# Attention scores and values in TensorE tiles of 64 rows by 32 columns, with two value banks and a ring of two score slots

## The reference, cut to what matters

```python
xn = layernorm(x)                                  # x: 4 x 2048 x 256
# two attentions of 8 heads of 16 columns, on two halves: xn itself and xn smoothed over time
scores = einsum('bshd,bthd->bhst', q, k) / sqrt(16)
o = einsum('bhst,bthd->bshd', softmax(scores), v)
x1 = layernorm(xh + o @ wo.T + bo);  x2 = the same on the smoothed half
y = concat([x1, x2])
first = layernorm(y + relu(y @ w_ff1.T + b_ff1) @ w_ff2.T + b_ff2)
second = relu(xn @ W1 + b1) @ W2 + b2
out = x + first + second
```

## Time and profile before

| | |
|---|---|
| time, median of 3 runs | 2540.47 us (2539.70 to 2545.86) |
| time of the profiled execution | 2538.24 us |
| its span in the trace | 2536.7 us |
| granted TensorE clock, mean | 0.991 |
| busy: PE, ACT, DVE, POOL | 2457.0, 2183.5, 1346.2, 327.5 us |
| exp (line 722) | 2048 instructions, 1904.7 us |
| values (line 1463), scores (line 1437), portions (line 1224, f16) | 1068.0, 621.4 and twice 214.7 us of PE |

### The profile page before, as it was taken

One profiled execution on the slowest core, in us unless ns is written; L12 is line 12 of the kernel. 1 busy time (PEld: TensorE's weight loads), 2 busy tenths in 40 slices (PEclk: granted clock), 3 DMA queues, 4 the chain that ended last, 5 costly groups with the idle time before them and its releaser, 6 DMA issues.

```text
span 2536.7 us, 66464 instructions
## 1 busy us (share of the span) xinstructions
PE 2457.0 (97%) x29057; PEld 965.5 (38%) x29057; DVE 1346.2 (53%) x3046; ACT 2183.5 (86%) x2419; POOL 327.5 (13%) x293
## 2 busy tenths in 40 slices
PE   6899999999999999999999999999999999999996
PEld 4233333336633333334653333333564333333354
DVE  5344445556744444555684444444677444445566
ACT  5899999986499999997569999999656999999952
POOL 1100110003400020000340002000053001100042
PEclk9999999999999999999999999999999999999998
DMA  8200220006110030000611004000151001200001
GB/s 221 80 10 10 37 40 12 6 6 128 51 60 10 10 61 10 10 6 12 138 50 44 10 10 61 10 10 6 51 99 51 10 10 27 44 10 10 6 30 43
DMA packets 49255, 95.94 MB, mean 38 GB/s; under 512 B 7468, under 2 KB 32044, under 8 KB 48572
## 3 DMA queue, kind: packets, MB, share of 16 engines
q1 hardware_dynamic: 42940, 77.12, 11.4%
q0 software_dynamic: 6016, 14.49, 4.1%
HBM read 57.45 MB, written 34.08 MB: 36 GB/s over the span
## 4 chain that ended last, share of the span: by engine, by line
PE 85%; DVE 10%; ACT 2%; issue 1%; POOL 1%; DMA 1%; SPq 0%; DVEq 0%; ACTq 0%; POOLq 0%
PE slot L1463 33%; PE slot L1437 19%; PE slot L1224 16%; PE slot L1496 6%; PE slot L1512 5%; DVE rden L857 2%; PE slot L1342 2%; DVE hid_one L889 1%; PE slot L1351 1%; DVE rs L771 1%; DVE rden L850 1%; DVE den L852 1%; POOL p_sb L601 1%; PE slot L1289 1%; ACT p_sb L722 1%
## 5 line engine op out<-in xcount | busy, mean ns | idle before, releaser
L722 ACT ACTIVATE p_sb<-slot 128x1024 f32<-128x1024 f32 x2048 | 1904.7, 1031 | 76.2 <-PE slot L1437 76.2
L1463 PE MATMUL slot<-p_sb,v_sb 128*17 128x512 f32 x8192 | 1068.0, 596 | 8.4 <-ACT p_sb L722 8.1
L1437 PE MATMUL slot<-q_st,k_st 50*128 50x512 f16 x4096 | 621.4, 382 | 5.4 <-ACT p_sb L722 3.2
L1437 PEld LDWEIGHTS slot<-q_st,k_st 50*128 50x128 f16 x4096 | 117.1, 94 | 874.3 <-ACT p_sb L722 870.6
L901 DVE SCALAR_TENSOR_TENSOR second<-slot,second 128x256 f32<-128x256 f32 x64 | 27.2, 425 | 593.0 <-PE slot L1224 593.0
L1463 PEld LDWEIGHTS slot<-p_sb,v_sb 128*17 128x17 f32 x8192 | 181.3, 96 | 226.3 <-ACT p_sb L722 208.2
L889 DVE TENSOR_SCALAR hid_one<-slot,b_grown 128x256 f32<-128x256 f32 x256 | 123.8, 483 | 238.6 <-PE slot L1224 236.5
L1224 PE MATMUL slot<-xt_parts,w_parts 128*32 128x256 f16 x6144 | 214.7, 274 | 13.0 <-DVE hid_one L889 13.0
L1224 PE MATMUL slot<-w_parts,hid_parts 128*32 128x256 f16 x6144 | 214.7, 274 | 0.0
L1224 PEld LDWEIGHTS slot<-xt_parts,w_parts 128*32 128x32 f16 x6144 | 140.7, 96 | 125.7 <-issue 95.4
L601 POOL TENSOR_TENSOR p_sb<-area,p_sb 128x512 f16<-128x512 f32 x128 | 149.1, 1166 | 291.1 <-ACT p_sb L738 284.8
(11 more groups left out here) (119 smaller groups left out, 1692.4 us busy)
## 6 DMA issues: line engine op xcount, KB each, us to landing
part_dram<-p_sb SPq DMA_DIRECT2D x16, 1024.0 KB, 4.2
xn<-x SPq DMA_DIRECT2D x16, 512.0 KB, 6.1
second<-x SPq DMA_DIRECT2D x32, 256.0 KB, 2.9
ffn_dram<-second SPq DMA_DIRECT2D x32, 256.0 KB, 2.0
area<-ffn_dram SPq DMA_DIRECT2D x16, 512.0 KB, 4.9
out<-area SPq DMA_DIRECT2D x15, 512.0 KB, 3.3
k_st<-part_dram SPq DMA_DIRECT2D x24, 256.0 KB, 12.0
k_st<-part_dram POOLq DMA_DIRECT2D x48, 128.0 KB, 5.1
```

Source lines behind the costliest of these rows:

```text
L722: act.activation(p_sb[:, n % 4, :], slot[n % 3][:, :], ACT.Exp, scale=0.25 / GROW ** 2).then_inc(exp_done, 1)
L1437: mm = pe.matmul(slot[at % 3][:, k * CHUNK:(k + 1) * CHUNK], k_st[rows_, pair, kt * P:(kt + 1) * P], q_st[rows_, pair, c_ * CHUNK:(c_ + 1) ...
L1463: mm = pe.matmul(o_bank[ROW * j:ROW * j + DK + 1, :], v_sb[:, a, kt, GH * g + j, :], p_sb[:, n % 4, (j % 2) * CHUNK:(j % 2 + 1) * CHUNK], ...
```

## The change

The scores and the values are cut into tiles of 64 rows by 32 columns. A score tile is made by eight matmuls (two row halves by four column groups of 32 keys) in place of two. The values of a kt are eight matmuls in place of four: for each of four heads one on keys 0 to 63 and one on keys 64 to 127, and the two halves go to two banks, `o_banks`, the two halves of slot 2. So slots 0 and 1 alone are the ring for scores: score tile n waits for exp n-2. PE's order in a kt becomes: first score tile of the next kt, portion, second score tile, values. `evict` must add the two banks: a copy of one to `rden`, an add of the other, which then frees the banks, and the shuffle from SBUF. In the prologue the third smoothing waits for `o_read`, and its order changes; in the last batch the first transpose waits for `o_read`.

The three small changes: the loads of the maxima for the next batch go from SP's queue to POOL's (`next_max`); the bias `b_ff2` is added on POOL ahead of `finish` (`bias_y`) and no longer in it; and the scaling in `finish` (line 949 to 956) is done in eight SCALAR_TENSOR_TENSORs of 256 columns instead of four small and two wide ones.

```diff
-            o_bank, side = slot[3][:, 0:CHUNK], slot[3][:, CHUNK:]
+            o_banks, side = [slot[2][:, r * CHUNK:(r + 1) * CHUNK] for r in range(2)], slot[3][:, CHUNK:]
...
-                        act.activation(p_sb[:, n % 4, :], slot[n % 3][:, :], ACT.Exp, scale=0.25 / GROW ** 2).then_inc(exp_done, 1)
+                        act.activation(p_sb[:, n % 4, :], slot[n % 2][:, :], ACT.Exp, scale=0.25 / GROW ** 2).then_inc(exp_done, 1)
...
-                    dve.stream_shuffle(o_sb[:, n % 2, :], o_bank, O_ROWS[n % 2]).then_inc(o_read, 1)
+                    step(dve.tensor_copy(rden[:, :], o_banks[0]))
+                    step.settle()
+                    dve.tensor_tensor(rden[:, :], o_banks[1], rden[:, :], ALU.add).then_inc(o_read, 1)
                     hold(dve, o_read, u + 2)
+                    step(dve.stream_shuffle(o_sb[:, n % 2, :], rden[:, :], O_ROWS[n % 2]))
+                    step.settle()
...
-                        step(dve.tensor_tensor(o_part, o_part, rows("b_ff2", CT // halves), ALU.add))
+                        rows_ = [o_all[:, t, :] for t in range(tiles.start, tiles.stop)]
+                        statistics(rows_)
+                        rsqrt(len(rows_))
+                        for i, row in enumerate(rows_):
+                            step(dve.scalar_tensor_tensor(row, row, mv[:, i, 0:1], c("gamma_ff"), ALU.subtract, ALU.mult))
...
+                        for i, row in enumerate(rows_):
+                            step(dve.scalar_tensor_tensor(row, row, rs[:, 1, i:i + 1], x4[:, tiles.start + i, :], ALU.mult, ALU.add))
...
+                        pe.wait_ge(exp_done, UNITS2 * STEPS * b + at - 1 + 3)
+                        pair = GH // 2 * g + n
+                        for r in range(P // ROW):
+                            for k in range(2):
+                                rows_ = slice(HALF * k, HALF * k + ROWS)
+                                mm = pe.matmul(slot[n][ROW * r:ROW * (r + 1), k * CHUNK:(k + 1) * CHUNK],
+                                               k_st[rows_, pair, kt * P + ROW * r:kt * P + ROW * (r + 1)],
+                                               q_st[rows_, pair, c_ * CHUNK:(c_ + 1) * CHUNK], start=True, stop=True, skip_group_check=True)
...
+                        for j in range(GH):
+                            n = 2 * kt + j // 2
+                            for r in range(2):
+                                rows_ = slice(HALF * r, HALF * (r + 1))
+                                mm = pe.matmul(o_banks[r][ROW * j:ROW * j + DK + 1, :], v_sb[rows_, a, kt, GH * g + j, :],
+                                               p_sb[rows_, n % 4, (j % 2) * CHUNK:(j % 2 + 1) * CHUNK],
+                                               start=(kt == 0), stop=(kt == TILES - 1), skip_group_check=True)
...
+                            if more:
+                                scores(at)
                             if kt in net_kts:
                                 (second_out_part if unit % 2 else second_hidden)(b, unit // 2, net_kts.index(kt))
                             if kt == PROJECTION_KT and unit > 0 and unit % 2 == 0:
                                 out_projection(b, unit - 1)
...
+                            if more:
+                                scores(at + 1)
+                            values(unit, kt)
```

More of the change, by code:

```diff
@@ L594, in first_y, with next_max, bias_y @@
                     pool.tensor_tensor(y4, y4, rows("beta", CT), ALU.add).then_inc(y_ready, 1)
+                def next_max(b):
+                    hold(pool, m_out, 16 * (2 * b + 1))
+                    fill_max(pool, 0, ALL_PAIRS, m_next_in)
+                def bias_y(b, cc):
+                    y4 = resid[:, CT * cc:CT * (cc + 1), :]
+                    pool.wait_ge(yt_rounded, CHUNKS * b + cc + 1)
+                    pool.tensor_tensor(y4, y4, rows("b_ff2", CT), ALU.add).then_inc(y_biased, 1)
                 def nets(b):
@@ L948, in finish @@
                             dve.wait_ge(ff_half_read, 1)
[L949 to L952 removed]
+                        rows_ = [o_all[:, t, :] for t in range(tiles.start, tiles.stop)]
[3 more added lines that the diff above has]
+                            step(dve.scalar_tensor_tensor(row, row, mv[:, i, 0:1], c("gamma_ff"), ALU.subtract, ALU.mult))
                         step.settle()
                         dve.wait_ge(back_in, 16 * (n + 1))
[L956 removed]
+                        for i, row in enumerate(rows_):
+                            step(dve.scalar_tensor_tensor(row, row, rs[:, 1, i:i + 1], x4[:, tiles.start + i, :], ALU.mult, ALU.add))
+                        step.settle()
+                        dve.sem_inc(o_ready if last_part else o_half_ready, 1)
                         if last_part:
@@ L1242, in second_hidden @@
                     h = HALVES * b + i
+                    if i == 0 and k == 0:
+                        pe.wait_ge(ff_read, CHUNKS * b + 2)
                     if k == 4 and i > 0:
@@ L1323, in smooth @@
                     def smooth(k):
+                        if k == 2 and before is not None:
+                            pe.wait_ge(o_read, UNITS2 * b + 1)
                         if k % 2 == 0:
@@ L1417, in attention, with scores @@
                 def attention(b):
-                    def scores(unit, kt):
+                    def scores(at):
+                        unit, kt, n = at // STEPS, at % STEPS // 2, at % 2
                         a, g, c_ = PAIRED_UNITS[unit]
-                        if kt == 0 and c_ == 0:
+                        if at % STEPS == 0 and c_ == 0:
                             if a == 1:
@@ L1427, in scores @@
                                 else:
-                                    hold(pe, q_next_in, 16 * Q_LOADS * b)
-                        for n in (2 * kt, 2 * kt + 1):
-                            at = STEPS * unit + n
-                            pe.wait_ge(exp_done, UNITS2 * STEPS * b + at - 2 + 3)
-                            if at == 2:
-                                pe.wait_ge(ff_read, CHUNKS * b + 1)
-                            for k in range(2):
-                                pair, rows_ = GH // 2 * g + n % 2, slice(HALF * k, HALF * k + ROWS)
-                                mm = pe.matmul(slot[at % 3][:, k * CHUNK:(k + 1) * CHUNK], k_st[rows_, pair, kt * P:(kt + 1) * P],
-                                               q_st[rows_, pair, c_ * CHUNK:(c_ + 1) * CHUNK], start=True, stop=True)
-                            mm.then_inc(scores_made, 1)
@@ L1441, in attention @@
-                    scores(0, 0)
-                    for unit, (a, g, c_) in enumerate(PAIRED_UNITS):
-                        u = UNITS2 * b + unit
+                                    hold(pe, q_next_in, 16 * 2 * len(Q_PART) * b)
+                                    hold(pe, m_next_in, 16 * 2 * b)
+                        pe.wait_ge(exp_done, UNITS2 * STEPS * b + at - 1 + 3)
[6 more added lines that the diff above has]
+                                               q_st[rows_, pair, c_ * CHUNK:(c_ + 1) * CHUNK], start=True, stop=True, skip_group_check=True)
@@ L1444, in attention @@
+                    scores(0)
+                    scores(1)
+                    for unit in range(UNITS2):
                         net_kts = OUT_KTS if unit % 2 else HIDDEN_KTS if unit else FIRST_HIDDEN_KTS
                         for kt in range(TILES):
-                            if kt + 1 < TILES:
-                                scores(unit, kt + 1)
-                            elif unit + 1 < UNITS2:
-                                scores(unit + 1, 0)
+                            at = STEPS * unit + 2 * kt + 2
+                            more = at < UNITS2 * STEPS
+                            if more:
+                                scores(at)
```

40 lines of the change are left out of this document (20 added, 20 removed).

## The result

The changed kernel takes 2667.49 us (median of four runs, 2663.57 to 2672.11) where the kernel before takes 2540.09 (2538.83 to 2545.86): a ratio of 1.0502, interval 1.0485 to 1.0520, so 127 us more. The profiled execution took 2664.47 us, which is 126.2 above that of before.

The account below looks back on a forecast made before the run. PE and ACT are both full in attention, with ACT stopping briefly for PE's score tiles. Terms 33 + 18 + 32 + 3.3 + 1.7 - 2.6 = +85 us on 2538.24 give 2623.6, median 2626; eight-in-ten range 2550 to 2700.

Parts of the forecast that it names:

- Faster: Attention: fewer layout changes end ACT's stops, new waits don't reach ACT, exps keep 0.917; 2474 us, chance 0.12.
- No change: Attention: free layout change, part of even boundary waits and all odd ones absorbed; 2540 within 8, chance 0.04.
- Tiles in turn: Score tiles: halves or column groups wait for each other's loads, 0.44 a tile; 2873 us, chance 0.08 wholly or in part.
- the forecast's own: Whole kernel: the range of the main forecast alone, 2580 to 2660 us, held with chance 0.76.
- Ring of two and order: Attention kts: the second score tile behind the portion makes ACT starve, 7.53 us per four kts against 7.40; +33 us.
- the walk: Step-by-step timing of PE and ACT through four kts (plain, portion, plain, portion), which gave a cycle of 7.53 us.
- estimate of 0.10: PE: a layout change between 128 by 32 portion and 64 by 32 score tile costs 0.10, nothing as lower bound.
- Wait for the eviction in odd units: Boundary into odd units: PE waits 0.56 for copy and add (1.41) before o_read, 32 times; +18 us.
- DVE's chain in even units: Boundary into even units: DVE's late shuffle moves hidden_half 1 and the third portion by 1.15, 28 times; +32 us.
- Prologue: Three prologues: DVE's state copies end later behind the eviction, PE's step goes 1.1 later each; +3.3 us.
- Last batch and tail: End of kernel: last-batch transposes wait for the eviction, +1.7 us; finish gets shorter by its new scaling, -2.6 us.
- well under 479: Attention stage: sign that the forecast is right, PE's busy time falling well below 479 us.

Follow-up runs that it names:

- e9: The kernel before with only the change's two-slot score ring and PE order, old tiles and old eviction: 2669.65 us, ratio 1.0500.
- e5: The kernel before with only the change's eviction (copy, combine, then shuffle), score tiles, order and ring as they were: 2592.45 us, ratio 1.0198.
- e1: The changed kernel with hidden_half 1 ahead of the first reciprocal and hidden_half 2 ahead of the second on DVE: 2645.7 us, ratio 1.0414.
- e2: The changed kernel with a third value bank, so that PE waits for the eviction's copy alone: 2652.67 us, ratio 1.0455.
- e4: The changed kernel with the stack refill's loads spread over the kts by waits on pv_done, not all at once: 2652.71 us, ratio 1.0441.
- e12: The changed kernel with the third portion of an even unit one kt later: 2658.22 us, ratio 1.0453.
- e3: The changed kernel with all four smoothing steps of the prologue ahead of the wait for the state: 2654.04 us, ratio 1.0439.
- e8: The changed kernel with third value bank, smoothing first, spread refill loads, and hidden_half 1 ahead of both reciprocals: 2604.78 us, ratio 1.0238.
- e11: The kernel before with the third portion of an even unit one kt later and the three small changes: 2526.24 us, ratio 0.9939.
- e7: The kernel before with only the three small changes (maxima loads on POOL, bias on POOL, scaling pairs in finish): 2534.73 us, ratio 0.9977.
- e6: The kernel before with hidden_half 1 ahead of both reciprocals on DVE: 2545.98 us, ratio 1.0017.
- e10: The kernel before with the third portion of an even unit one kt later: 2529.32 us, ratio 0.9944.

## Why the prediction was right, and where its sizes were off

The direction and the mechanism were right: all three rivals fall. *Faster* needed copy and add in under 0.87, and they took 1.41. *No change* needed a free change of layout, and it took 0.10. *Tiles in turn* needed 0.44 per score tile, and it took 0.22. The sum was +85 and the profiled difference is 126: the time lies inside the wide range of 2550 to 2700, and above the forecast's own of 2580 to 2660. By its terms:

- **Ring of two and order**, +33: the cycle is 7.57 and not 7.53. (In the walk the first late exp is late by 0.03 and not 0.05; the end at 5.17, with which it goes on, is right.) Before, an odd unit of four cycles was 29.63, so 7.41 each: 256 x 0.16 = +41. The two parts in it are now apart: order and ring alone make the cycle 7.96 (e9), the equal tiles bring it to 7.57. The estimate of 0.10 for the change between portion and score tile held (0.77 for 0.67). The Trainium skill, "TensorEngine Tiling (Array Packing)", Tiling Modes, says that a change of mode drains the engine whichever the modes; the rows of e9 and of the changed kernel agree, 0.10 to 0.12 for each pair that they show.
- **Wait for the eviction in odd units**, +18: 30.86 - 4 x 7.57 = 0.58 a unit, 32 x 0.58 = +19.
- **DVE's chain in even units**, 1.15 each and +32: an even unit takes 32.96 (median), which is 2.68 above its four cycles of 7.57; before it was 30.88 - 29.63 = 1.25 above them. So 1.43 each, 28 x 1.43 = +40. This step was mis-sized. The same eviction in the old order costs 1.18 (e5), which is the 1.15 of the prediction (757.11 - 756.00 is 1.11; a gap of 0.04 behind the shuffle makes it 1.15). The other 0.25 is there only with the change. DVE's chain from the copy to `hidden_half` 1 is as long there as in e5 (7.64 and 7.65), but PE stops at the third portion for 1.22 and not for 0.96. From the values that the eviction lets go to this portion it is 798.33 - 792.10 = 6.23, less the stop 5.01; in e5 776.87 - 770.63 = 6.24, less the stop 5.28. So PE is there 0.27 sooner: one score tile of 0.22, not two, stands ahead of the portion. The prediction moved the portion and the tile behind it by the 1.15 of DVE, and did not count that PE comes sooner. No run changes the order alone at this place.
- **Prologue**, +3.3: +19. This step failed. The delay of DVE's copies is nearly as forecast (1.33 of stop; 1.4 a prologue in e5), but 1.1 us of lateness was taken as 1.1 us of time. The one prologue without a fall of the clock grew by 2.3; the two with one took 7.6 more each; 3 x 2.3 + 2 x 7.6, less the 3.2 of the fall in the kernel before, are the 19. What makes the falls so long is not settled. With the stop and the new order of the smoothing (the changed kernel, e1, e2, e4, e12) the clock fell in 10 of 15 prologues, for 13.7 or 17.1 us; with the same stop and the old order (e5) in 2 of 3, for 6.8; without the stop (e3, e8) in 3 of 6, for 10.2. So the order, which the prediction counted as nothing, seems to have a part in it.
- **Refill**, not in the sum: +9. The prediction counted what the matmuls take to run and not that 20480 more of them, with their loads, must be fetched (160 more packets of 16 KB). e4 shows the cause by taking away the burst in front of the fetch.
- **Last batch and tail**, +1.7 and -2.6: +1.2. Up to PE's last matmul the tail is 2.9 longer: the clock stays low for 6.8 us at its start where it was 3.4 before, which is about 1.7, and the rest is the eviction's. Behind that matmul it is 1.7 shorter, and 1.2 and 1.4 in the kernels with the small changes alone (e11, e7): the 2.6 was too much, since a pair of SCALAR_TENSOR_TENSORs takes 0.88 and pairs have gaps of up to 0.29 ahead of them.

These are 41 + 19 + 40 + 19 + 9 + 1 = 129, 3 above the measured 126. The 41 counts the 16 cycles of the batches' first units with +2.6, but those units became 0.8 shorter together. Every term was too small, and no error made up for another: that the time still lies in the wide range is owed to its width.

One sign was wrong too: PE's busy time was to be "well under 479", and it is 480.01. Against e9, which has the same order and ring, it did fall, by 515.71 - 480.01 = 36 us a stage. But busy time counts a matmul to its modelled end: of the 0.33 us between the end of S1's stream (837.22 + 0.22) and S2 (837.77) the profile shows only 0.15 as idle. Small stops hide in busy time; starts show them.

What stays open: why the clock falls. A stop of PE stood ahead of it in the changed kernel, but the same stop also passed without a fall, and in e8 and in the kernel before the clock fell without one.

## What to carry to other kernels

When a change saves PE work by giving a second thing two PSUM banks, cost what those banks did before: here a third score slot and the freedom of order that it gave were worth 130 us, the equal tiles 100, and emptying two banks one after the other another 50. A wait that one removes from an in-order engine tends to reappear at the next dependence (e1, e2, e6, e12); what helped was to move the waiting portion itself by one kt (e10; in the changed kernel, e12, it left a stop of 0.61 at the next portion). Multiply instructions only after a look at the fetch queue, and at what DMA bursts it shares the engines with.

## What the runs showed of the hardware

Instruction fetches share the DMA engines with the kernel's own loads: behind 14 loads that filled them for about 10 us, a 16 KB fetch came late and PE stood for 3.3 us. Loads spread over the unit took that away. The granted clock fell to half for 6.8 to 17 us in prologues whose lengths else agree within 0.4 us in one kernel, and a prologue with a stop of 1.3 us of PE grew by up to 10. It fell in 10 of 15 prologues of one order with this stop, and in 4 of 18 of the kernel before and its variants without a stop (e6, e7, e9, e10, e11). Eight matmuls of 64x32 tiles stream in the 0.22 us that two of 64x128 took, and sixteen of 64x17 in the 0.86 of eight of 128x17, their loads hidden.
